# A depthwise convolution, attention and MLP kernel in exact fp32 pieces: tap layout, order of the tensor engine's step in attention, and the edges of the MLP's chunks

## What is computed

```python
# layer 0: attention with a depthwise convolution added to the queries
local  = batch_norm(conv7x7_depthwise(x))
q,k,v  = split(layernorm(x_flat) @ qkv_w.T + qkv_b)          # 8 heads of 48, 2304 tokens
q      = q + layernorm(local_flat)
out    = softmax(q @ k.T * 48**-0.5) @ v
x      = x_flat + out @ proj_w.T + proj_b
# layer 1: convolution, layer norm, MLP with global response normalisation
y = conv7x7_depthwise(x) + dw_b
y = gelu(layernorm(y) @ w1 + b1)                             # 1536 wide
y = grn_g * (y * gx / mean(gx)) + grn_b + y                  # gx: norm of y over the pixels
out = x + y @ w2 + b2
```

## Time and profile before

| what | value |
|---|---|
| median of 3 runs | 5748.92 us (5747.1 to 5751.15) |
| profiled execution, its own time | 5749.09 us |
| its span in the trace | 5747.1 us |
| PE busy with matmuls | 5415.1 us, 94% |
| ACT busy | 3952.3 us, 69% |
| DVE busy | 3777.1 us, 66% |
| POOL busy | 2084.5 us, 36% |
| mean granted clock of PE | 0.979 |

### The profile page before, as it was taken

The page is one execution under the profiler, slowest core; times in us unless marked ns, Lnnn a source line. Parts: engine busy times, 40 slices in busy tenths (PEclk is TensorE's granted clock), DMA queues, the critical chain, the costliest instruction groups (busy, mean ns, idle before and its releaser), DMA issues. The chain is left out here.

```text
span 5747.1 us, 95795 instructions
## 1 busy us (share of the span) xinstructions
PE 5415.1 (94%) x31248; PEld 5149.3 (90%) x31248; DVE 3777.1 (66%) x5909; ACT 3952.3 (69%) x5653; POOL 2084.5 (36%) x1028
## 2 busy tenths in 40 slices
PE   7879989999999999999999999999878889999999
PEld 6779978999999999999999999999877778888888
DVE  4456658777777777777777777777444445555645
ACT  6655546888888888888888888888626754434343
POOL 0003334666666556666655666666300000000000
PEclk9999998999999999999999999999999999999999
DMA  4458862213131221312222131221274531111111
GB/s 121 117 140 267 258 207 38 50 30 55 31 55 31 43 43 30 55 31 49 36 37 49 31 55 30 43 43 30 83 261 113 117 64 38 42 38 42 41 34 46
DMA packets 639648, 419.84 MB, mean 73 GB/s; under 512 B 490353, under 2 KB 620081, under 8 KB 629553
## 3 DMA queue, kind: packets, MB, share of 16 engines
q1 hardware_dynamic: 611312, 379.21, 28.5%
q10 hardware_dynamic: 27840, 34.37, 1.7%
HBM read 252.72 MB, written 160.43 MB: 72 GB/s over the span
## 5 line engine op out<-in xcount | busy, mean ns | idle before, releaser
L845 POOL TENSOR_TENSOR a_e_lo<-a_e_full,a_e_hi 128x768 fp32r<-128x768 f32 x864 | 1924.7, 2228 | 1343.0 <-ACT a_e_hi L855 1290.3
L918 DVE TENSOR_REDUCE a_mx_part<-a_ps_m 128x2 f32<-128x768 f32 x1700 | 1628.4, 958 | 743.2 <-PE a_ps_m L980 715.5
L886 ACT ACTIVATE a_e_full<-a_ps_s 128x768 f32<-128x768 f32 x1728 | 1405.2, 813 | 497.2 <-PE a_ps_s L998 431.4
L855 ACT ACTIVATE a_e_hi<-a_e_full 128x768 fp32r<-128x768 f32 x1728 | 1449.0, 839 | 0.0
L998 PE MATMUL a_ps_s<-a_q,a_k_hi 113*128 113x384 f32 x3456 | 1171.2, 339 | 8.3 <-issue 6.6
L998 PE MATMUL a_ps_s<-a_q,a_k_lo 113*128 113x384 f32 x3456 | 1167.6, 338 | 0.0
L1012 PE MATMUL a_ps_o<-a_e_hi,a_v 128*97 128x384 f32 x3456 | 919.6, 347 | 5.1 <-ACT a_o_t L861 3.8
L980 PE MATMUL a_ps_m<-a_k_hi,a_q 112*128 112x384 f32 x3400 | 883.4, 341 | 33.7 <-DMA a_q<-q_lo 26.4
L1012 PE MATMUL a_ps_o<-a_e_lo,a_v 128*97 128x384 f32 x3456 | 884.3, 337 | 7.6 <-issue 7.6
L911 DVE TENSOR_TENSOR a_e_lo<-a_e_full,a_e_hi 128x768 fp32r<-128x768 f32 x864 | 831.9, 963 | 36.6 <-ACT a_e_hi L855 36.6
L998 PEld LDWEIGHTS a_ps_s<-a_q,a_k_hi 113*128 113x128 f32 x3456 | 651.3, 188 | 38.7 <-issue 17.6
(11 more groups left out here) (146 smaller groups left out, 7271.3 us busy)
## 6 DMA issues: line engine op xcount, KB each, us to landing
local<-c_res ACTq DMA_DIRECT2D x192, 168.0 KB, 2.3
v<-n_v SPq DMA_DIRECT2D x24, 1152.0 KB, 6.3
a_v<-v SPq DMA_DIRECT2D x32, 864.0 KB, 14.5
a_k_hi<-k_hi SPq DMA_DIRECT2D x63, 432.0 KB, 6.8
a_k_lo<-k_lo SPq DMA_DIRECT2D x63, 432.0 KB, 15.5
c_band_raw<-in_taps SPq DMA_DIRECT2D x768, 24.0 KB, 2.4
c_x_raw<-in_x_conv SPq DMA_DIRECT2D x96, 144.0 KB, 2.2
n_xc<-in_x SPq DMA_DIRECT2D x24, 576.0 KB, 6.3
```

The costliest lines, as they stand in the source:

```text
L845: pool.tensor_tensor(e_lo[:, e], e_full[:, e], f32(e_hi[:, e]), ALU.subtract).then_inc(lo_pool, 1)
L855: act.activation(e_hi[:, slot(par, n)], e_full[:, slot(par, n)], ACT.Copy).then_inc(e_hi_made, 1)
L886: act.activation(e_full[:, slot(par, n)], ps_s[:, n % 2, :, 0:CHUNK], ACT.Exp, scale=float(HD) ** -0.5).then_inc(e_made, 1)
L918: dve.tensor_reduce(mx_part[:, par, t, 2 * pair:2 * pair + 2], max_bank(h, u), AX.X, ALU.max).then_inc(mx_red[u % 2], 1)
```

## The change

1. **Taps.** The buffer `band_raw` is laid out [3, channel, 6, 32] in place of [3, 6, channel, 32]. So each of the four transfers of a group writes 192 contiguous numbers in a partition where it wrote six runs of 32 (128 bytes each). ACT and DVE read the buffer through a permuted view and write `band_hi` and `band_lo` in the old layout.
2. **PE's step in attention.** `products` of n-4 is called first in step n, then `scores(n)`, `maxima(n)`, and `combine` or `turn`. Nothing else changes in the stage: ACT, DVE, POOL and SP keep their order.
3. **The MLP.** (a) ACT writes `x_hi` of tiles 0 and 2 of the next chunk before the Gelu of unit 11, in place of all three tiles after it; DVE copies tile 1 (`x_mid`). (b) DVE makes the three `x_lo` before the sum of squares of unit 11, not after it. (c) The raw input of chunk 1 of a batch goes to a free part of `hid` and is issued in chunk 4 of the batch before; `io` gets the raw input from chunk 2 on. PE's `tokens` of chunk 1 now waits for the last `y_made` of the batch before.

```diff
-        band_raw = sb("band_raw", [P, 3, 6, PC, PS])
+        band_raw = sb("band_raw", [P, 3, PC, 6, PS])
...
-                    sp.dma_start(band_raw[rows, k, :, c, :], taps[g, rows].rearrange("p (o s) -> p o s", s=PS)).then_inc(tap_in[k], 16)
+                    sp.dma_start(band_raw[rows, k, c].rearrange("p o s -> p (o s)"), taps[g, rows]).then_inc(tap_in[k], 16)
...
-                act.activation(band_hi[:, k], band_raw[:, k], ACT.Copy).then_inc(band_hi_made, 1)
+                act.activation(band_hi[:, k], band_raw[:, k].rearrange("p c o s -> p o c s"), ACT.Copy).then_inc(band_hi_made, 1)
...
                 for n in range(STEPS):
+                    if prev and n < LAG:
+                        products(h - 1, 1 - par, n - LAG + STEPS)
+                    if main and n >= LAG:
+                        products(h, par, n - LAG)
                     if main:
                         scores(h, par, n)
...
                         turn(h, par, 1)
-                    if prev and n < LAG:
-                        products(h - 1, 1 - par, n - LAG + STEPS)
-                    if main and n >= LAG:
-                        products(h, par, n - LAG)
...
-        first_raw = hid[:, 0:CT, CHUNK:2 * CHUNK]
+        early_raw = [hid[:, 0:CT, (c + 1) * CHUNK:(c + 2) * CHUNK] for c in range(2)]
         def raw_of(u):
-            return io if u % NCH else first_raw
+            return io if u % NCH > 1 else early_raw[u % NCH]
...
+                    if c == NEXT_X and b + 1 < nb:
+                        raw((b + 1) * NCH + 1)
...
+            def x_highs(u):
+                at_least(act, x_free, u)
+                for t in (0, 2):
+                    x_high(u, t)
             def up(b):
                 for c in range(NCH):
                     u = b * NCH + c
-                    if c:
-                        act.wait_ge(x_free, u)
-                        for t in range(CT):
-                            x_high(u, t)
                     for f in range(FT):
                         n = c * FT + f
+                        if c + 1 < NCH and f == FT - 1:
+                            x_highs(u + 1)
                         act.wait_ge(h_done, b * NF + n + 1)
...
+            def x_mid(u):
+                at_least(dve, x_free, u)
+                dve.wait_ge(full_made, u * 3 + 2)
+                dve.tensor_copy(x_hi[:, 1], full[:, 1]).then_inc(x_mid_made, 1)
...
+                        if c + 1 < NCH and f == FT - 1:
+                            x_mid(u + 1)
                         dve.wait_ge(h_made, b * NF + n + 1)
...
+                        if c + 1 < NCH and f == FT - 1:
+                            for t in range(CT):
+                                x_low(u + 1, t)
...
                 pe.wait_ge(raw_in, landed(u))
+                if u % NCH == 1:
+                    at_least(pe, y_made, u // NCH * NC3)
```

More of the change, by code:

```diff
@@ L244, in band @@
                 at_least(dve, conv_done, g - 2)
-                dve.tensor_tensor(band_lo[:, k], band_raw[:, k], f32(band_hi[:, k]), ALU.subtract).then_inc(band_lo_made, 1)
+                dve.tensor_tensor(band_lo[:, k], band_raw[:, k].rearrange("p c o s -> p o c s"), f32(band_hi[:, k]), ALU.subtract).then_inc(band_lo_made, 1)
             def body(g, k):
@@ L1197, in mlp_stage @@
             "to_tok", "stats", "sd_made", "rs_made", "normed", "to_ch", "full_made", "eps_made"))
[L1198 removed]
+        x_free, x_hi_made, x_mid_made, x_lo_made = sem("x_free"), sem("x_hi_made"), sem("x_mid_made"), sem("x_lo_made")
         h_done, h_made, sq_made = sem("h_done"), sem("h_made"), sem("sq_made")
@@ L1270, in raw @@
                     sp.wait_ge(to_tok, u * 3)
-                if c == 1:
+                if c == 2:
                     at_least(sp, stored, b * NCH * 16)
@@ L1296, in _ @@
             for b in range(nb):
-                if b:
-                    raw(b * NCH + 1)
                 for c in range(2, NCH):
@@ L1349, in down @@
                         affine((b + 1) * NCH, NEXT_CH[f])
-                    if b + 1 < nb and c == NEXT_X and f in X_AT:
+                    if b + 1 < nb and c == NEXT_X and f in X_AT and X_AT[f] != 1:
                         x_high((b + 1) * NCH, X_AT[f])
@@ L1383, in normal @@
                                   ALU.subtract, ALU.mult).then_inc(normed, 1)
+            def x_mid(u):
+                at_least(dve, x_free, u)
+                dve.wait_ge(full_made, u * 3 + 2)
+                dve.tensor_copy(x_hi[:, 1], full[:, 1]).then_inc(x_mid_made, 1)
             def x_low(u, t):
-                dve.wait_ge(x_hi_made, u * CT + t + 1)
-                at_least(dve, h_done, u * FT)
+                if t == 0:
+                    at_least(dve, h_done, u * FT)
+                if t == 1:
+                    dve.wait_ge(x_mid_made, u + 1)
+                else:
+                    dve.wait_ge(x_hi_made, u * 2 + t // 2 + 1)
                 dve.tensor_tensor(x_lo[:, t], full[:, t], f32(x_hi[:, t]), ALU.subtract).then_inc(x_lo_made, 1)
@@ L1410, in up @@
                     u = b * NCH + c
-                    if c:
-                        for t in range(CT):
-                            x_low(u, t)
                     for f in range(FT):
@@ L1469, in down @@
                         if ahead is not None and c == NEXT_X and f in X_AT:
+                            if X_AT[f] == 0:
+                                x_mid(ahead)
                             x_low(ahead, X_AT[f])
@@ L1480, in _ @@
             dve.wait_ge(par_in, 96)
+            x_mid(0)
             for t in range(CT):
@@ L1513, in up @@
                         for t in range(CT):
-                            if f == 0 and j != 1:
-                                pe.wait_ge(x_lo_made if j else x_hi_made, u * CT + t + 1)
+                            if f == 0 and j == 2:
+                                pe.wait_ge(x_lo_made, u * CT + t + 1)
+                            if f == 0 and j == 0:
+                                if t == 1:
+                                    pe.wait_ge(x_mid_made, u + 1)
+                                else:
+                                    pe.wait_ge(x_hi_made, u * 2 + t // 2 + 1)
                             last = pe.matmul(ps_h[:, f % 3, 0:CHUNK], wp[:, t, f * P:(f + 1) * P], xp[:, t],
```

## The result

| | before | changed |
|---|---|---|
| median of 3 runs, us | 5748.92 | 6362.03 (6361.35 to 6366.59) |
| ratio, 95% interval | 1 | 1.1068 (1.1043 to 1.1094) |
| profiled execution, its span, us | 5749.09, 5747.1 | 6361.35, 6359.4 |
| mean granted clock | 0.979 | 0.957 |
| attention, PE's first to last matmul, us | 3261 | 3966 |

The change costs 613 us; 6176 were forecast (+427), and the range ended at 6265. The sum of the stages in the two traces shows where it went: from the start to PE's first matmul behind the first convolution -33, from the last of the projection to the first of the MLP -29, MLP -34, projection +3 (not looked into), attention +705. The kernel before and the changed one ran three times each; of the experiments, those with a range ran four times and the others once.

A forecast was written before the change was run, and what follows sets the result against it. PE was taken to bound the kernel, busy 94% of the span and without reserve in attention. 5749.1 + 336 (chunks' first products) + 197 (odd products) - 72 (taps) - 34 (MLP) = 6176 us, range 6090 to 6265.

The forecast's parts named there:

- The first product of a chunk: Attention: PE waits 1.91 us for ACT's copy, plus 0.08 restart, at 191 places; +336 us.
- The odd products: Attention: DVE's low part comes 0.34 us late, 0.42 with restart, for 15 products a head; +197 us.
- POOL's even products: Attention: POOL's piece looks nearly late but stays hidden; 0 us, some +30 if POOL ran 0.2 us slower.
- The clock: Rival, attention: ten matmuls behind each long stall run at 1.2 GHz, another +336 us, total 6512; chance 0.06.
- The taps: Both convolutions: cheaper issues of 0.43 us bring a group to 3.18 us; -72 us, bounds 0 to -100.
- the loop through ACT: Convolutions: finish, band, x_hi and x_lo take 6.26 us for two groups, a floor of 3.13 us a group.
- The MLP: MLP stage: -10 us at 20 chunk edges and -24 us at three batch edges, -34 together.
- 20 edges: MLP chunk edges: unit 1 starts 0.5 us earlier, x_lo is late next; -10 us, bounds 0 and -20.
- the three batch edges: MLP: waits of 6.57 us for raw input go, plus some 1 us each; -24 us, bounds -18 and -30.

The follow-up runs named there:

- e6_lag5: Changed kernel with LAG = 5 in place of 4: every product gets its fifth step back, ACT's copy moves along; 6103.4 us.
- e8_fill: Changed kernel plus nine matmuls of 352 columns, results unread, ahead of PE's wait for ACT's copy at each chunk's first product; 6186.7 us.
- e5_copy_early: Changed kernel with ACT's copy of a finished attention chunk moved one step earlier; 5913.3 us.
- e1_order: Kernel before with only the new order of PE's step in attention; 6470.8 us against 5741.9 on the same chip.
- e3_mlp: Kernel before with only the MLP's part of the change; 5705.1 us against 5741.9 on the same chip.
- e7_both: Changed kernel with LAG = 5 and ACT's copy one step earlier, products still called first; 5698.1 us.

## Why the prediction was right or wrong

**The first product of a chunk: right.** 191 stalls of 1.91 us with 0.08 of restart were forecast. Above, PE stands ready at 909.48 and starts at 911.31, 1.83 us, and the product then takes 0.77; there are 190 such waits on L861. The count, the releaser and the size agree within 5%. e6_lag5, which has only these stalls, confirms the price: a chunk at the full clock takes 18.4 us where it takes 16.6 to 16.7 in the kernel before, 1.8 more (1.76 forecast).

**The odd products: right in mechanism, nearly in size.** 0.34 us and 15 in a head were forecast, two of them eased. The view of waits has 13 in a head put down to DVE, and the timeline of a head has two more, shorter, idle times. In the stretch above the product comes 0.75 us behind the start of M where 0.35 is its pace, 0.40 late. DVE's piece took longer to reach PE (907.51 to 907.66) than the 0.06 us that I took over from ACT's copy. At the full clock a head takes 117.4 us with both kinds of stall (e8_fill) and about 110.5 with the long ones alone (six chunks of e6_lag5), so the short ones cost 6.9 us a head where 6.15 were forecast.

**POOL's even products: right.** No wait of PE on POOL is among the large ones of the changed kernel.

**The clock: wrong, and this is the error of the total.** The step that failed is the term of the clock: the sum put it at nothing. It stood among the rivals with 0.06, priced at +336 us, and the forecast and its range left it out. Measured, it is some 165 us (108 stretches of 1.53 us) of the 186 by which the time exceeds the forecast. Ten more are the taps' term and 3 the projection.

What I set against it was the convolution's 1.00 at 16% of idle time "in small gaps". That was misread. The 22.6 us of idle time in that window are 37 pieces of up to 2.20 us, and the mean of a window hides what follows a single one. The trace of the kernel before does have rows for an idle time of 2 us. Here is one in the first convolution (2.03 us idle before the first row), with the window behind it, in which the clock reads 0.51; then, as a contrast, matmuls and a window behind an idle time of 2.20 us, where it reads 1.00.

```profile
102.48 1.26 PE L294 MATMUL c_acc<-c_x_hi,c_band_hi 128*128 128x336 f32 x6 [2.03 <-issue]
103.54 1.88 PE L294 MATMUL c_acc<-c_x_lo,c_band_hi 128*128 128x336 f32 x6
105.22 1.83 PE L294 MATMUL c_acc<-c_x_hi,c_band_lo 128*128 128x336 f32 x6
106.88 1.11 PE L294 MATMUL c_acc<-c_x_hi,c_band_hi 128*128 128x336 f32 x6
...
103.40:106.80 3.40, 3.40 (x14) 3.40 (x13) 1.57 (x2) 0.95 (x2) 0.00 (x0) 0.51 0.54 128
...
148.78 1.18 PE L294 MATMUL c_acc<-c_x_hi,c_band_hi 128*128 128x336 f32 x6 [2.20 <-issue]
149.79 1.10 PE L294 MATMUL c_acc<-c_x_lo,c_band_hi 128*128 128x336 f32 x6
150.73 1.10 PE L294 MATMUL c_acc<-c_x_hi,c_band_lo 128*128 128x336 f32 x6
...
149.00:152.40 3.40, 3.03 (x19) 2.78 (x19) 1.53 (x3) 2.02 (x3) 0.00 (x0) 1.00 0.46 119
```

From 103.54 to 106.88 twelve matmuls take 3.34 us where they take 1.88 at the full clock: 1.46 us lost, close to the 1.5 that a stretch costs in attention. In the two convolutions of that trace four of the five idle times of 2.0 to 3.4 us within the groups are followed by such a stretch, and none of the nine of 1.6 to 1.8 us. The stall of 1.91 us lay between the two. So the rows did not decide it, but they gave a price of 1.46 us for each of 191 places, 279 us at most. That called for a larger chance and a range that reaches higher.

The rival's own price was too high: not each of the 191 stalls is followed by a stretch at 1.2 GHz, but at most 108 are. The Trainium skill (TensorE: Matmul & The Clock Gate, A second HAM failure mode: psum-queue depth-cycling) tells of a kernel whose TensorE idles between groups of matmuls and pays for it in clock. The changed kernel agrees with it at long idle times, 0.95, and e5_copy_early doesn't at short ones, 1.00.

**The taps: the mechanism right, the term too large.** -72 were forecast, -62 measured (-33 and -29). Part of the -33 may be spread: with its code unchanged the first convolution takes 348 us in e1_order and 345 in e3_mlp, where it takes 352 here. An issue takes 0.42 us; 0.43 was forecast. The timeline of the changed kernel, which answers to the earlier trace rows:

```profile
156.66 0.35 SPq L180 DMA_DIRECT2D c_x_raw<-in_x_conv  x1
...
157.05 1.84 SPq L186 DMA_DIRECT2D c_band_raw<-in_taps  x4
...
160.60 0.87 ACT L203 ACTIVATE c_band_hi<-c_band_raw 128x768 fp32r<-128x768 f32 x1
```

Four issues take 1.84 us (2.51 before), and in this round ACT takes the taps without a wait. The window shows 3.26 us a group (790 matmuls are 43.9 groups in 143 us) where I had 3.18, from 3.60. Many groups stand at 2.89 and 3.38 in turn, which is the 3.13 of the loop through ACT; single groups of 4.1 to 4.9 us remain and make up the difference. I counted them as gone. The Trainium skill (DMA: Bandwidth & Descriptors, Anatomy of one DMA) calls descriptor generation small, but for transfers that GpSimd issues. These are issued by SP, so the 0.42 us for an issue of the same bytes that took 0.6 doesn't speak for or against it.

**The MLP: right in the sum and in both parts.** -34 forecast, -34 measured. The timeline of the changed kernel at the edge of a chunk; it answers to the earlier trace rows:

```profile
5363.84 0.68 PE L1540 MATMUL m_ps_h<-m_x_lo,w_hi 128*128 128x384 f32 x3
5364.03 0.94 ACT L1319 ACTIVATE m_x_hi<-m_full 128x384 fp32r<-128x384 f32 x2 [0.46 <-PE m_ps_h L1540]
...
5365.48 1.50 DVE L1400 TENSOR_TENSOR m_x_lo<-m_full,m_x_hi 128x384 fp32r<-128x384 f32 x3 [1.02 <-ACT m_hid L1334]
...
5367.31 0.69 PE L1540 MATMUL m_ps_h<-m_x_hi,w_hi 128*128 128x384 f32 x3
```

From the last three of unit 11 to unit 1 it is 3.47 us in place of 3.93, so 0.46 each for 20 edges, 9 us (10 forecast), and it is x_lo that is late now, waiting for the Gelu as forecast. The remaining 25 us are put down to the three batch edges (24 forecast): the three waits of some 6.6 us for raw input, 20 us, are gone from the trace, and the last 5 are only the rest.

## What to carry to other kernels

In a software pipeline over several in-order engines, the place of a call within the step is part of the distance to its suppliers. Turning PE's step by one call took one step from each supplier of the product, and each supplier's own order (what stands before it on its engine) decides the price; read for each how long after PE's last contribution it is ready, and compare that with the new place. Where a stall of 2 us is to recur in a stage whose PE was never idle, put the lower clock into the sum and not among the accidents. Look for single idle times of that length anywhere in the trace and read the clock just behind each: the mean of a long window read 1.00 in the same stage.

## What the hardware showed that I had not expected

**Idle time of one kind costs clock, of another it doesn't.** 4% of PE's time in waits of 0.25 us left the clock at 1.00 (e5_copy_early). Waits of some 1.7 us, one every 18 to 21 us at some 190 places, lowered it to 0.95 to 0.96 (the changed kernel, e6_lag5), and matmuls whose results nobody reads, put there, saved 175 us (e8_fill).

**DVE's and POOL's subtractions of the low parts seem to get in each other's way, and the one that comes second pays.** In the first heads of e7_both DVE's (L911) took 2113 ns on average and from its fourth head on 949, for the same shape. Groups of L911 in the windows 900 to 1100 and 1200 to 1400 us, then the timeline at 998 and at 1402 us:

```profile
L911 DVE TENSOR_TENSOR a_e_lo<-a_e_full,a_e_hi 128x768 fp32r<-128x768 f32 x43 | 90.9, 2113 | 0.0
...
L911 DVE TENSOR_TENSOR a_e_lo<-a_e_full,a_e_hi 128x768 fp32r<-128x768 f32 x54 | 51.2, 949 | 0.0
```

```profile
998.75 1.82 POOL L845 TENSOR_TENSOR a_e_lo<-a_e_full,a_e_hi 128x768 fp32r<-128x768 f32 x1 [2.85 <-ACT a_e_hi L855]
...
999.16 2.22 DVE L911 TENSOR_TENSOR a_e_lo<-a_e_full,a_e_hi 128x768 fp32r<-128x768 f32 x1
...
1402.56 2.28 POOL L845 TENSOR_TENSOR a_e_lo<-a_e_full,a_e_hi 128x768 fp32r<-128x768 f32 x1 [1.23 <-ACT a_e_hi L855]
...
1402.16 0.95 DVE L911 TENSOR_TENSOR a_e_lo<-a_e_full,a_e_hi 128x768 fp32r<-128x768 f32 x1
```

At 998 POOL is first and done at 1000.57; DVE, which came 0.41 us later, ends 0.81 after that, almost its full duration. At 1402 DVE is first and undisturbed, and POOL takes 2.28 in place of 1.82. In the first case the next reduction, and with it M on PE, is late: 46 us in three heads, until it ends by itself. The first head of the kernel before, at 105.9 us in place of 99.9, has L911 at 1419 ns in the window 900 to 960 us, perhaps a shorter case of the same. That the two take turns is what the durations suggest; no run here isolates it, nor what ends the phase.
